# Values of both attentions kept in slot order in device memory; typed second pass summed in PSUM

## What is computed

```python
# relational attention, for each edge type r
e = leaky_relu(Qn[tgt] @ a_q + Kn[src] @ a_k)       # Qn = x @ WQ[r], Kn = x @ WK[r], Vn = x @ WV[r]
attn = softmax of e over the edges of type r with the same tgt
h_prime += segment_sum(where(edge_type == r, Vn[src] * attn, 0), tgt)
# typed attention, 8 heads of 16; Q, K, V by node type, K turned by a matrix of the edge type
scores = (Q[dst] * kt).sum(-1) / sqrt(16) * mu[:, edge_type].T
smax = segment_max(scores, dst);  ex = exp(scores - smax[dst]);  den = segment_sum(ex, dst)
w = ex / (den[dst] + 1e-10);      out = segment_sum(w * V[src], dst)
```

## Time and the profile before

| | us |
|---|---|
| median of 3 runs | 6560.58 (6554.14 to 6580.65) |
| the profiled execution | 6499.4 |
| its span in the trace | 6497.7 |
| PE / PEld / DVE / ACT / POOL busy | 3728.7 / 3244.4 / 2938.5 / 822.6 / 3273.6 |
| mean granted PE clock | 0.656 of full speed |

### The profile page before, as it was taken

One profiled execution on the slowest core, in us unless ns is written; L12 is line 12 of the kernel. 1 busy time (PEld: TensorE's weight loads), 2 busy tenths in 40 slices (PEclk: granted clock), 3 DMA queues, 4 the chain that ended last, 5 costly groups with the idle time before them and its releaser, 6 DMA issues. The chain is left out here.

```text
span 6497.7 us, 81708 instructions
## 1 busy us (share of the span) xinstructions
PE 3728.7 (57%) x19254; PEld 3244.4 (50%) x19255; DVE 2938.5 (45%) x9185; ACT 822.6 (13%) x1860; POOL 3273.6 (50%) x3327
## 2 busy tenths in 40 slices
PE   0000889866666466653644443677775666546665
PEld 0000788855655355542624332466665566346664
DVE  5000666643433333333794434266673444343334
ACT  0000111120111011120100000111111111311112
POOL 4775555536664466603004663166665566036662
PEclk9999777765555555565555555855555666768887
DMA  5232444432222222223402222211111111111112
GB/s 187 74 77 76 118 113 113 116 61 62 66 64 51 60 64 65 64 48 102 112 3 56 68 67 34 73 41 40 41 35 39 41 42 42 11 43 52 53 52 34
DMA packets 394236, 415.69 MB, mean 64 GB/s; under 512 B 230871, under 2 KB 296473, under 8 KB 394137
## 3 DMA queue, kind: packets, MB, share of 16 engines
q0 software_dynamic: 105984, 211.53, 13.1%
q1 hardware_dynamic: 233240, 141.69, 7.8%
q10 hardware_dynamic: 54912, 61.36, 3.5%
HBM read 325.69 MB, written 88.62 MB: 64 GB/s over the span
## 5 line engine op out<-in xcount | busy, mean ns | idle before, releaser
L603 POOL DMA_INDIRECT ring<-table_gine,idx x1248 | 1220.5, 978 | 962.0 <-DVE mraw L641 407.8
L1518 PE MATMUL ps<-msg,oh 128*128 128x128 f32 (+2 forms) x4160 | 919.0, 389 | 476.8 <-DVE HA L641 425.2
L1518 PEld LDWEIGHTS ps<-msg,oh 128*128 128x128 f32 x4160 | 819.6, 289 | 544.4 <-DVE HA L641 419.9
L641 DVE TENSOR_TENSOR mraw<-ps,ring 128x512 f32<-128x512 f32 x520 | 358.4, 689 | 1076.2 <-remote 671.7
L641 DVE TENSOR_TENSOR HA<-HA,ps 128x128 f32 (+2 forms) x2080 | 598.3, 288 | 249.3 <-DVE HA L641 124.9
L622 POOL DMA_INDIRECT ring<-table_rel,idx x368 | 350.9, 954 | 628.4 <-PE ps L1663 458.7
L603 POOL DMA_INDIRECT ring<-table_keys,idx x416 | 459.2, 1104 | 406.2 <-SPq L184 202.4
L1527 PE MATMUL ps<-wt,ear 64*128 64x128 f32 x2496 | 599.4, 410 | 60.9 <-DMA ear<-edge_attr_T 44.0
L603 POOL DMA_INDIRECT ring<-table_msg,idx x416 | 399.7, 961 | 464.4 <-SPq L184 215.9
L1527 PEld LDWEIGHTS ps<-wt,ear 64*128 64x128 f32 x2496 | 511.9, 300 | 130.0 <-issue 120.3
L603 POOL DMA_INDIRECT ring<-table_values,idx x416 | 400.3, 962 | 293.5 <-DVE msg L641 135.6
(11 more groups left out here) (288 smaller groups left out, 6103.1 us busy)
## 6 DMA issues: line engine op xcount, KB each, us to landing
ear<-edge_attr_T SPq DMA_DIRECT2D x312, 128.0 KB
oh<-slot_rows ACTq DMA_DIRECT2D x104, 256.0 KB
slot_records<-msg SPq DMA_DIRECT2D x32, 650.0 KB, 11.2
arena<-slot_records SPq DMA_DIRECT2D x104, 200.0 KB
edge_attr_T<-arena ACTq DMA_DIRECT2D x104, 192.0 KB
ring<-table_gine,idx POOLq DMA_INDIRECT x1248
ear<-slot_rows ACTq DMA_DIRECT2D x104, 128.0 KB
arena<-in_edge_attr SPq DMA_DIRECT2D x50, 250.0 KB
```

Of the source, the lines that this page charges most:

```text
L603: pool.indirect_dma_start(out=ring[:, k % 4, j, 0:width], out_offset=None, in_=table[:, :], in_offset=bass.IndirectOffsetOnAxis(ap=idx[:, ...
L641: return V.tensor_tensor(o, x, y, op)
L1518: ins = M.matmul(out_of(t, j), oh[:, t.s4, j, :], x, start=True, stop=True)
```

## The change

Three edits, with one store between them, `slot_values`, in which each batch's value rows stand in slot order (256 KB for a batch).

Relational attention. POOL issues all 416 gathers from the start into HA, 12 batches deep, and waits only for the landing of the batch four back and for the write-out of the batch twelve back; SP writes each batch to `slot_values`; in the attention loop ACT's queue reads it back into `ring`, two batches behind the slot rows that it already loads.

Typed tables and first pass. One table `table_keys_values` with rows of 1 KB replaces two; the values are written for each of the 5 edge types of a node. The first pass gathers key and value as one row, and SP writes the value half to `slot_values`.

Typed second pass. No gathers: SP reads the batches back in order. ACT's queue loads slot rows, DVE makes transposed bf16 one-hots of them, and the maxima, split in three bf16 parts (MXP), are looked up with them. PE adds messages and weights directly in PSUM, 8 f32 matmuls a batch, with 7 matmuls of 512 columns before and after the loop; the PSUM tiles that DVE added up are gone, and so are the transposes.

```diff
-        tab2k = dram("table_keys", [NPAD * NREL, D])
-        tab2v = dram("table_values", [NPAD, D])
+        vals = dram("slot_values", [NB, P, B * D])
+        tab2 = dram("table_keys_values", [NPAD * NREL, 2 * D])
...
-        vpre = HA[:, 0:PRE * B * D].rearrange("p (k j d) -> p k j d", k=PRE, j=B)
+        vdeep = HA[:, 0:DEEP * B * D].rearrange("p (k j d) -> p k j d", k=DEEP, j=B)
...
+        kvring = aren[:, NPAD:NPAD + 4 * B * 2 * D].rearrange("p (s j w) -> p s j w", s=4, j=B)
+        MXP = T[3][:, 0:NBLK * 3 * NHEAD // 2].bitcast(BF16).rearrange("p (b i g) -> p b i g", b=NBLK, i=3)
...
+        densum = psf[:, NPAD:NPAD + NBLK * NHEAD].rearrange("p (b g) -> p b g", b=NBLK)
...
+            for k in range(NB):
+                sp.wait_ge(qa.gath[k % 4], 16 * B * (k // 4 + 1))
+                if k >= 4:
+                    sp.wait_ge(values_out[k % 4], 16 * (k // 4))
+                sp.dma_start(vals[k], vdeep[:, k % DEEP].rearrange("p j d -> p (j d)")).then_inc(values_out[k % 4], 16)
...
+            t2b = tab2.rearrange("(b p r) (w d) -> b p r w d", p=P, r=NREL, w=2)
+            for b in range(NBLK):
+                sp.wait_ge(pn_free, QV_EVACS + b + 1)
+                sp.dma_start(t2b[b][:, :, 1, :], T3[4][:, b, :].unsqueeze(1).to_broadcast([P, NREL, D])).then_inc(t_out, 16)
...
             for b in range(NBLK):
                 sp.wait_ge(vals_rdy, 2 * (b + 1))
-                sp.dma_start(t2v[b], kwb[:, b % 2, :]).then_inc(keys_out[b % 2], 16)
+                sp.dma_start(t2v[b][:, :, 0, :], kwb[:, b % 2]).then_inc(keys_out[b % 2], 16)
...
-            table(tab2v, T3[4], 4)
...
+            join.to("tr_values")
+
+            for k in range(NB):
+                sp.wait_ge(qm.gath[k % 4], 16 * B * (k // 4 + 1))
+                sp.wait_ge(values_out[k % 4], 16 * (NB // 4 + k // 4))
+                sp.dma_start(vals[k].rearrange("p (j d) -> p j d", j=B), kvring[:, k % 4, :, D:2 * D]).then_inc(values_out[k % 4], 16)
+            join.to("tr_zero")
+            for k in range(NB):
+                sp.wait_ge(values_out[k % 4], 16 * (NB // 4 + k // 4 + 1))
+                if k >= 4:
+                    sp.wait_ge(qt["messages"], k - 3)
+                sp.dma_start(ring[:, k % 4, :, 0:D], vals[k].rearrange("p (j d) -> p j d", j=B)).then_inc(values_in[k % 4], 16)
...
-                if k >= PRE + 4:
-                    pool.wait_ge(qa["sums"], k - 3)
+                if k >= 4:
+                    pool.wait_ge(qa.gath[k % 4], 16 * B * (k // 4))
+                if k >= DEEP:
+                    pool.wait_ge(values_out[k % 4], 16 * ((k - DEEP) // 4 + 1))
                 for j in range(B):
...
+                    pool.indirect_dma_start(
+                        out=vdeep[:, k % DEEP, j, :], out_offset=None, in_=tab1[:, :],
+                        in_offset=bass.IndirectOffsetOnAxis(ap=idx5[:, k * B + j:k * B + j + 1], axis=0)).then_inc(qa.gath[k % 4], 16)
             join.to("tr_values")
-            gathers(qm, "scores", tab2k, D, idx5)
-            join.to("tr_zero")
-            gathers(qt, "messages", tab2v, D, idx1)
+            for k in range(NB):
+                if k >= 4:
+                    pool.wait_ge(qm["scores"], k - 3)
+                    pool.wait_ge(values_out[k % 4], 16 * (NB // 4 + k // 4))
+                for j in range(B):
+                    pool.indirect_dma_start(
+                        out=kvring[:, k % 4, j, :], out_offset=None, in_=tab2[:, :],
...
-            ch(V.memset(AG[:, :], 0.0))
+            split([MXP[:, :, i, :] for i in range(3)], MX[:, :, :], mx_rest)
             join.to("tr_zero")
...
+            def tr_dst_onehots(t):
...
+                dve.wait_ge(drin[t.s4], t2.u * 16 + 16)
...
+                    dve.wait_ge(qt["node"], t.n - 1)
+                V.tensor_scalar(oT[:, t.h, 0], drow[:, t.s4], iota_p, None, ALU.is_equal).then_inc(qt["onehotT"], 1)
+
+            ch_tl = Steps(dve, qt["chain"], 2)
+
             def tr_logit(t):
+                ch_tl.start(t.n)
                 dve.wait_ge(qt["node"], t.n + 1)
...
-                tt(small3[:, t.s4, 0:B * NHEAD], score[:, bass.ds(t.k * (B * NHEAD), B * NHEAD)],
-                   ps[:, 2 + t.h, 0:B * NHEAD], ALU.subtract).then_inc(qt["logits"], 1)
+                own = small4[:, t.s4, 0:B * NHEAD]
+                ch_tl.step(V.reduce_sum(own.rearrange("p (j g) -> p j g", j=B),
+                                        ps[:, 7, 0:B * 3 * NHEAD].rearrange("p (j i g) -> p j g i", j=B, i=3), AX))
+                yield
+                ch_tl.done()
+                dve.sem_inc(qt["picked"], 1)
+                ch_tl.step(tt(small3[:, t.s4, 0:B * NHEAD], score[:, bass.ds(t.k * (B * NHEAD), B * NHEAD)], own, ALU.subtract))
+                yield
+                ch_tl.done()
+                dve.sem_inc(qt["logits"], 1)
             def tr_message(t):
                 dve.wait_ge(qt["exp"], t.n + 1)
...
-
-            run(dve, [(5, acc_pair(qt, agg2, W2N)), (3, tr_message), (2, tr_logit), (0, onehots(qt["onehot"], qt["sums"], oh))])
...
+                dve.wait_ge(values_in[t.s4], Batch(t.r, t.s, 1).u * 16 + 16)
+                tt(msg[:, t.s4, :, 0:D].rearrange("p j (g d) -> p j g d", g=NHEAD),
+                   ring[:, t.s4, :, 0:D].rearrange("p j (g d) -> p j g d", g=NHEAD),
+                   msg[:, t.s4, :, D:W2N].unsqueeze(3).to_broadcast([P, B, NHEAD, HD]), ALU.mult).then_inc(qt["messages"], 1)
+
+            run(dve, [(4, tr_message), (2, tr_logit), (1, tr_dst_onehots), (0, onehots(qt["onehot"], qt["sums"], oh))])
+            dve.wait_ge(pe_made, tr_sums)
+            den = densum
...
+            def values_back(t):
+                act.wait_ge(values_out[t.s4], t.u * 16 + 16)
+                if t.late(4):
+                    act.wait_ge(qa["sums"], t.n - 3)
+                act.dma_start(ring[:, t.s4, :, 0:D], vals[bass.ds(t.k, 1)].rearrange("a p (j d) -> p (a j) d", j=B)).then_inc(values_in[t.s4], 16)
+            run(act, [(4, att_exp), (0, att_in), (2, values_back)])
...
+            def tr_rows_in(t):
+                if t.late(4):
+                    act.wait_ge(qt["onehotT"], t.n - 3)
+                act.dma_start(drow[:, t.s4], slotrow[1:2, bass.ds(t.k * B, B), :].rearrange("w t s -> w (t s)")
+                              .to_broadcast([P, B * P])).then_inc(drin[t.s4], 16)
+            run(act, [(3, tr_exp), (0, tr_rows_in)])
...
+                pe.wait_ge(values_in[t.s4], t.u * 16 + 16)
...
                 for j in range(B):
                     ins = M.matmul(psf[:, bass.ds(blocks[j] * D, D)], oh[:, t.s4, j, :],
-                                   vpre[:, t.k, j, :] if early else ring[:, t.s4, j, 0:D], start=False, stop=False)
+                                   ring[:, t.s4, j, 0:D], start=False, stop=False)
                 ins.then_inc(qa["sums"], 1)
-            run(pe, [(6, att_sums), (2, att_lookups)], lead=PRE // 4 + 2)
+            run(pe, [(6, att_sums), (2, att_lookups)])
...
-            run(pe, [(4, sums(qt, W2N, pair(W2N), ready="messages")),
-                     (1, node_rows(qt, rows_at(MX, NHEAD), lambda t, j: ps[:, 2 + t.h, j * NHEAD:(j + 1) * NHEAD], own, "logits")),
-                     (0, turn_onehot(qt, own))])
+            for z in range(7):
+                n = min(512, NPAD + NBLK * NHEAD - z * 512)
+                M.matmul(ps[:, z, 0:n], b2row[0:1, :], wt[0:1, 0:n], start=True, stop=False)
+
+            def tr_lookups(t):
+                pe.wait_ge(qt["onehotT"], t.n + 1)
+                if t.late(1):
+                    pe.wait_ge(qt["picked"], t.n)
+                blocks = blocks_of(pe, PE, t)
+                for j in range(B):
+                    ins = M.matmul(ps[:, 7, j * 3 * NHEAD:(j + 1) * 3 * NHEAD], oT[:, t.h, 0, j * P:(j + 1) * P],
+                                   MXP[:, bass.ds(blocks[j], 1), :, :].rearrange("p a i g -> p (a i g)"), start=True, stop=True)
+                ins.then_inc(qt["node"], 1)
+
+            def tr_into(t):
+                pe.wait_ge(qt["onehot"], t.n + 1)
+                pe.wait_ge(qt["messages"], t.n + 1)
+                pe.sem_inc(pe_go, 1)
+                blocks = blocks_of(pe, PE, t)
+                for j in range(B):
+                    M.matmul(psf[:, bass.ds(blocks[j] * D, D)], oh[:, t.s4, j, :], msg[:, t.s4, j, 0:D], start=False, stop=False)
+                    ins = M.matmul(psf[:, bass.ds(blocks[j] * NHEAD + NPAD, NHEAD)], oh[:, t.s4, j, :], msg[:, t.s4, j, D:W2N],
+                                   start=False, stop=False)
+                ins.then_inc(qt["sums"], 1)
+            run(pe, [(5, tr_into), (2, tr_lookups)])
+            for z in range(7):
+                n = min(512, NPAD + NBLK * NHEAD - z * 512)
+                ins = M.matmul(ps[:, z, 0:n], b2row[0:1, :], wt[0:1, 0:n], start=False, stop=True)
+            ins.then_inc(pe_made, 1)
```

More of the change, by code:

```diff
@@ L44 @@
 HEAD = 16
-PRE = 12
+DEEP = 12
 G = 400
@@ L251, in late, with run @@
```

(2 more changed lines are left out.)

56 lines of the change are left out of this document (19 added, 37 removed).

## The result

The changed kernel takes 6747.89 us in the median (6739.35 to 6757.86, 4 runs) against 6562.81 for the kernel before: ratio 1.0279, 95% interval 1.0253 to 1.0305. The forecast was 6495, with a range to 6640. It lies 108 us above that range.

What follows compares the result with a forecast made beforehand. No engine's total was taken as the bound, but handoffs, with gathers holding back PE's results. Terms +178, +15, +12 and -270 on the profiled 6499.4 made 6434, plus 61 to the median: 6495 us, range 6080 to 6640.

Steps and rivals of the forecast that it cites:

- So PE sets the pace and the clock decides: Typed second pass: PE bounds each batch at 3.6 us, so 405 us against 675, a gain of 270.
- the prediction's lower bound for the gain: Typed second pass: PE at 4.8 us a batch, leaving a gain of 145 us.
- The relational attention: Lookups through attention loop: 237 us gained without gathers in the loop, 415 lost to late lookups, a net loss of 178.
- The lateness L: Lookups beside the gathers: held at some 30 us a batch, ending 415 us late; bounds 0 and 440.
- Tables and first pass: Typed tables: +15 us for writing 16 MB instead of 8; typed first pass: +12 for doubled rows and write-outs.
- Rival A: Relational attention: gathers hide for nothing, lookups not late, 480 us off the execution, so 6081 us; chance 0.20.
- Rival B: Relational gathers: POOL's pauses let PE's results through, lookups about 220 us late, so 6300 us; chance 0.22.
- Rival D: Typed second pass: PE stays at 1.2 GHz and is the bound, 4.8 us a batch, so 6621 us; chance 0.20.
- The 5.0 us a batch of the attention loop before: Attention loop of the kernel before: 520 us for 104 batches, close to the 5.0 us that four gathers make.
- a clock of 0.51 to 0.61: Granted PE clock in every stage with PE 46 to 73% busy, cited for PE staying at 1.2 GHz.

Runs made afterwards that it cites:

- the pairs: Changed kernel with second-pass messages three and sums four batches back, POOL also waiting for the landing after every second relational gather: 6235.81 us, 0.9477 of the kernel before.
- the order of the second pass: Changed kernel with typed second-pass messages three batches back instead of four, PE's sums four instead of five: 6548.14 us, 0.9935 of the kernel before on chip 0.
- typed edits with the mended order: Kernel before with only the typed edits, second-pass messages three batches back and sums four back: 5564.44 us, 0.9787 of the kernel before on chip 13.

## Why the prediction was wrong

**The step that failed is the second pass**, "So PE sets the pace and the clock decides". Neither did. The step summed PE's and DVE's work per batch, took the longer and never asked whether the two can lie beside each other. The lags of the diff and the depth of `oh` answer that without any run: what DVE multiplies in turn k is what its one-hots of turn k wait to see summed. The pass took 5.78 us a batch, above even the 4.8 of the prediction's lower bound for the gain. With the messages one turn earlier it takes 392 us where the forecast had 405, though by other terms, and that nearness is luck: the clock stayed at 0.50 with PE busy for 99% of the window, where I had read 0.73 from the first edge convolution, and PE's batch costs 3.5 us at that clock, where I had summed overlapping groups to 4.8. The gap of the term is 204 us on the stage table. The forecast, moved by it, is 6699 us, near the 6748 measured, and on its side.

**The relational attention was right in its mechanism and off in one size.** The loop gained 243 us for a forecast of 237. The lateness L was 472 for 415. The gathers took 1.34 us each and not 1.25, which is 38 us; the hold went on 26 us past them, where I had 6; and a batch took 44.8 us and not 30, though the earlier trace rows already had 43.18 for the later one, which cost three batches or 6 us. I had set the upper bound at 440, by gathers of 520 us and no hold behind them; both were too short.

**Tables and first pass**: +2 for +15, and +8 for +12. The value rows and their write-out more than double the DMA share (0.17 to 0.40), and hide as reckoned, as far as profiles that differ by 20 us can say.

**Rival A** had the right mechanism on two chips of five, though not its time: it put the change 480 us ahead, and on chip 10 it was 20, for the second pass stood in lockstep there too. What I took for a fixed price of the kernel goes with the chip that ran it, and one profile doesn't show that. **Rival B**, pauses that let PE through, is what the pairs then showed; in the stream of the changed kernel POOL's longest pause was 1.6 us. **Rival D** had the right side and the right clock, 0.50, but not the bound: PE was busy for 385 of 595 us, and at that clock it can do a batch in 3.5.

**Two readings** in the prediction were off without entering the sum. The 5.0 us a batch of the attention loop before divides 520 us by 104 batches, but the window holds 88 or 89, so it is 5.9. And the stages with PE at 46 to 73% busy have a clock of 0.51 to 0.61 only if the row of the typed tables in the earlier trace rows is passed over: 70% busy and 0.91.

That the order of the second pass is the whole difference between 1.028 and 0.9935 is shown: the pass is 226 us shorter on chip 0, and on chip 10 the two kernels, run on the same chip, differ by 222. Where the typed half loses on chips without late handoffs is argued only: typed edits with the mended order gain 121 us there (0.9787), the order is worth 222 to 226, so the typed half as changed costs some 100; the kernel before's passes were never profiled on such a chip.

## What to carry to other kernels

Where two engines feed each other through a ring, write down for one turn which batch each stage works on and which batch its wait names, before any durations: if producer and consumer of one batch stand in the same turn, their times add, and a lag moved by one can be worth more than the edit under study. A long unbroken run of one engine's background work is a price to be measured beside every engine that hands over there, not only the one that is busiest, and for some time behind it. And a stage time can belong to the chip: the same kernel took 14% less time on two of them, and the verdict on the change went from slower to the same.

## What the runs showed of the hardware

On chips 0, 9 and 3, PE's results are late beside a stream of gathers that POOL issues without a break (0.94 us busy, 0.30 between): 2.80 us a matmul, whether there are 16 or 4 in a batch (chip 0) or 8 (chip 9); chip 3 shows it in the kernel before, with lookups of 289 us. It stays with 4 to 8 gathers on their way in place of 16 to 20, goes when POOL waits for each landing (41 gathers beside the lookups in 212 us), and nearly goes with pairs. It outlasts a stream of 416 gathers by 26 us in the changed kernel and by 27 with the gathers behind the lookups, and the 64 early gathers of the kernel before by 7. Something that a stream piles up and that needs a pause to drain would fit all of this; that is argued, and what it would be, no run shows.

On chips 10 and 13 it isn't there, at a DMA share of 0.84 and back-to-back issue. The prediction cited the Trainium skill's SBUF — State Buffer, Who interferes with whom, that PE and ACT never wait on anyone. Chips 10 and 13 agree with that, with lookups of 227 us beside the gathers on chip 10; chips 0, 9 and 3 don't, with up to 44.8 us a batch. That section is about SBUF ports, and whether these are involved isn't shown. What makes the chips differ stays open.

A granted clock of 0.50 with PE busy for 367 of 369 us was not expected either: the earlier trace rows has 0.73 at 89% and 0.91 at 70%. The stretch of 0.50 is the lower of the two levels, 1.2 GHz, throughout, on chips of both kinds.
